# A decoder layer on one core: a prologue in halves and pieces, weight splits moved to GpSimd, and sixteen products of zeros at the start

## The reference

```
x = _layernorm(x + attn(x))            # 32 heads of 16, causal
x = _layernorm(x + xattn(x, ctx))      # 32 query heads in 8 groups, head size 128, rotary
x = _layernorm(x + ffn(x))             # 4-bit weights, 1376 wide, silu gate, result in float16

# attn: q, k, v = x @ W.T + b
scores = einsum('bhqd,bhkd->bhqk', q, k) / sqrt(16), causal
out = einsum('bhqk,bhkd->bhqd', softmax(scores), v) @ Wo.T + bo
# xattn: q = rope(query @ wq); k = rope(ctx @ wk); v = ctx @ wv
w = softmax(where(mask, einsum('bhgqd,bhkd->bhgqk', q, k) / sqrt(128), -1e9))
out = einsum(w, v) @ wo
# ffn: gate * sigmoid(gate) * up, gate = x @ Wg, up = x @ Wu, then @ Wd
```

## Time and profile before

| | us |
|---|---|
| median of 3 runs | 992.58 (988.86 to 994.84) |
| the profiled execution | 994.55 |
| its span in the trace | 992.7 |
| PE busy | 912.0 (92%) |
| DVE busy | 729.7 (74%) |
| ACT busy | 463.7 (47%) |
| POOL busy | 365.3 (37%) |

### The profile page before, as it was taken

One profiled execution on the slowest core, in us unless ns is written; L12 is line 12 of the kernel. 1 busy time (PEld: TensorE's weight loads), 2 busy tenths in 40 slices (PEclk: granted clock), 3 DMA queues, 4 the chain that ended last, 5 costly groups with the idle time before them and its releaser, 6 DMA issues.

```text
span 992.7 us, 17835 instructions
## 1 busy us (share of the span) xinstructions
PE 912.0 (92%) x6552; PEld 520.5 (52%) x6552; DVE 729.7 (74%) x1190; ACT 463.7 (47%) x1335; POOL 365.3 (37%) x330
## 2 busy tenths in 40 slices
PE   3876899888789999999999999999998989999997
PEld 2555677544345555545555555555554544444443
DVE  5685989877577877859787687787788655898343
ACT  3665788641145545535554454554545533333100
POOL 2152122103345444534554455446556230231011
PEclk9997999889999999999999999999999999999999
DMA  6634442210001101012002003004111010220001
GB/s 198 222 133 145 154 119 65 84 67 1 1 1 44 41 25 42 24 43 85 23 2 85 22 2 106 2 32 154 49 48 47 4 48 1 95 96 1 11 33 43
DMA packets 50535, 59.48 MB, mean 60 GB/s; under 512 B 5037, under 2 KB 35728, under 8 KB 50448
## 3 DMA queue, kind: packets, MB, share of 16 engines
q1 hardware_dynamic: 50448, 58.33, 18.2%
HBM read 51.96 MB, written 6.36 MB: 59 GB/s over the span
## 4 chain that ended last, share of the span: by engine, by line
PE 66%; DVE 13%; issue 9%; POOL 4%; ACT 4%; DMA 2%; SPq 1%; POOLq 0%; DVEq 0%; ACTq 0%
PE bank L292 19%; PE bank L293 19%; PE bank L294 19%; DVE rsin L873 3%; PE bank L1271 2%; ACT prob L691 1%; PE bank L1162 1%; POOL res L463 1%; DVE nmax L791 1%; PE bank L1261 1%; PE bank L1260 1%; PE bank L1259 1%; PE bank L1255 1%; DVE pTl L765 1%; ACT prob L575 1%
## 5 line engine op out<-in xcount | busy, mean ns | idle before, releaser
L470 POOL TENSOR_TENSOR rot<-rcos,rsin 128x512 f32<-128x512 f32 x80 | 101.3, 1266 | 123.2 <-DVE rsin L873 123.1
L482 POOL TENSOR_TENSOR pnrm<-prob,rden 128x512 f32<-128x512 f32 x64 | 66.5, 1040 | 125.0 <-DVE rden L933 124.9
L292 PE MATMUL bank<-aTh,xqh 128*128 128x512 f16 x256 | 98.2, 384 | 6.4 <-DVE aTl L765 3.7
L293 PE MATMUL bank<-aTl,xqh 128*128 128x512 f16 x256 | 98.1, 383 | 0.0
L530 ACT ACTIVATE pTh<-bank 128x512 f16<-128x512 f32 x128 | 78.5, 613 | 41.8 <-PE bank L1271 28.1
L294 PE MATMUL bank<-aTh,xql 128*128 128x512 f16 x256 | 97.9, 383 | 0.0
L294 PE MATMUL bank<-xoh,o2l 128*128 128x512 f16 x256 | 97.8, 382 | 0.0
L293 PE MATMUL bank<-xol,o2h 128*128 128x512 f16 x256 | 97.7, 382 | 0.0
L292 PE MATMUL bank<-xoh,o2h 128*128 128x512 f16 x256 | 97.6, 381 | 0.0
L610 ACT CAST q2h<-rot 128x512 f16<-128x512 f32 x64 | 39.5, 617 | 116.4 <-POOL rot L470 116.3
L575 ACT ACTIVATE prob<-bank,ebias 128x128 f32<-128x128 f32 x256 | 73.6, 382 | 42.3 <-DVE ebias L794 41.9
(11 more groups left out here) (159 smaller groups left out, 2454.0 us busy)
## 6 DMA issues: line engine op xcount, KB each, us to landing
tst<-tables SPq DMA_DIRECT2D x11, 768.0 KB, 5.5
xqs<-in_xwq SPq DMA_DIRECT2D x8, 1024.0 KB, 6.7
xos<-in_xwo SPq DMA_DIRECT2D x8, 1024.0 KB, 5.5
qst<-in_fq SPq DMA_DIRECT2D x11, 384.0 KB, 3.4
kstk<-stack SPq DMA_DIRECT2D x48, 64.0 KB, 2.3
qstk<-stack SPq DMA_DIRECT2D x24, 128.0 KB, 2.6
stT<-in_xT SPq DMA_DIRECT2D x4, 512.0 KB, 7.2
stT<-in_ctxT SPq DMA_DIRECT2D x1, 2048.0 KB, 8.1
```

The lines of the kernel that those rows point to most:

```text
L292: pe.matmul(out_ap, ah, bh, start=first, stop=False)
L293: pe.matmul(out_ap, ah, bl, start=False, stop=False)
L470: nc.gpsimd.tensor_tensor(rot[:, r % 2, :], rcos[:, r % 2, :], rsin[:, r % 2, :], ALU.add).then_inc(rope_rot, 1)
L482: nc.gpsimd.tensor_tensor(pnrm[:, v % 2, :].rearrange("p (h k) -> p h k", h=QH), prob[:, v % 2, :].rearrange("p (h k) -> p h k", h=QH), rd ...
```

## The change

The diff makes five groups of edits.

1. **Prologue.** The transposed x is loaded and split in halves of 512 columns (`load_x`, `x_split_hi`, `x_split_lo`), and the weights of keys, queries and values each have their own semaphore, so the first key products wait for the key weights and for one quarter of the first half at a time. The bias columns are loaded from ACT's queue. For block 0, ACT writes the high part of keys and queries straight from PSUM beside qkf, DVE makes the low part (`first_split_lo`), SP takes the keys through the scratch tensor and ACT the queries. The loads of the tables and the mask are issued after the keys of block 0, and DVE computes the tables and mbias in step 1 and no longer in step -8.
2. **Zero products.** POOL clears one half of pTh, and PE multiplies it sixteen times, 128 by 128 by 512, before its first step. The first `p1_hi` steps wait for them.
3. **Weight splits on POOL.** `split_piece` is three POOL instructions: scale the float32 tile in place, convert to the high part, subtract for the low part. POOL does so for the self attention's third and fourth weight sets (6 pieces), for wo (4), for the cross attention's query, key and value weights of groups 0 and 1 (12) and its output weights of group 0 (4): 26 pieces. ACT and DVE lose one instruction each for every piece. POOL's eight additions of bo move to steps 24 to 31, and its splits of keys and queries are interleaved by step.
4. **Self attention.** ebias is computed by ACT just before the exponentials and no longer by DVE; DVE's split of the values comes at the end of the same step, one step earlier than before.
5. **End of the cross attention.** The four transposes of res stand one step later, `gate_up(0)` one step earlier.

PE's list at the start, before: the products of keys wait for everything at once.

The diff, cut to what the list above names:

```diff
+IDLE = 16
...
-    plan += [(END - 6 + b, "t", (1, b)) for b in range(4)]
+    plan += [(END - 5 + b, "t", (1, b)) for b in range(4)]
...
-    qkv = {0: [24, 26, 28, 30, 32, 34], 1: [38, 40, 42, 44, 46, 48]}
-    out = {0: [50, 52, 54, 55], 1: [T0 + 2, T0 + 3, T0 + 4, T0 + 5]}
+    qkv = {0: [26, 28, 29, 30, 34, 36], 1: [38, 42, 44, 45, 46, 50]}
+    out = {0: [52, 53, 54, 58], 1: [T0 + 2, T0 + 3, T0 + 4, T0 + 5]}
...
+W1_SLOT = {(2, 0): 4, (2, 1): 5, (2, 2): 6, (3, 0): 20, (3, 1): 21, (3, 2): 22}
+WO1_SLOT = {0: 10, 1: 12, 2: 13, 3: 14}
+POOL_QKV, POOL_OUT = (0, 1), (0,)
...
-EARLY_GU = {END: [0], END + 1: [1], END + 3: [2], END + 5: [3]}
+EARLY_GU = {END - 1: [0], END + 1: [1], END + 3: [2], END + 5: [3]}
...
-GU_USE = {0: END + 1, 1: END + 2, 2: END + 4, 3: END + 6}
+GU_USE = {0: END, 1: END + 2, 2: END + 4, 3: END + 6}
...
+            def keep_first_keys():
+                sp.wait_ge(first_lo, 1)
+                for i, src in enumerate((k1h, k1l)):
+                    sp.dma_start(stack_d[0, i], src[:, :]).then_inc(k1_out, 16)
+
+            def bring_keys(j):
...
+                keep_rows(j, 0, k1_out, 2 * j - 1)
+                keep_rows(j, 2, q1_out, 2 * j)
+                if j >= 2:
+                    sp.wait_ge(s_psum, TILES1 * (j - 1))
+                bring_keys(j)
                 sp.wait_ge(q1_out, 32 * (j + 1))
...
+            def load_x(half):
+                cols = slice(half * HALF, (half + 1) * HALF)
...
+                    sp.dma_start(stT[:, k, cols], xT[k * P:(k + 1) * P, cols]).then_inc(x_in[half * NK + k], 16)
...
+            load_first_w1(0, wkT)
+            load_x(0)
+            load_first_w1(1, wqT)
+            load_first_w1(2, wvT)
+            load_x(1)
+            for dst, src in ((ident, ident_d), (tri_f, tri_d)):
+                sp.dma_start(dst[:, :], src).then_inc(early_in, 16)
             load_w1(1)
+            keep_first_keys()
+            bring_keys(0)
...
-            stack_rows(0)
+            sp.wait_ge(xT_lo, NHALF * NK)
             sp.dma_start(stT[:, :, :], ctxT.rearrange("(k p) t -> p k t", p=P)).then_inc(ctx_in, 16)
             stack_rows(1)
...
+            nc.gpsimd.memset(pTh[:, 0, :], 0.0).then_inc(idle_zero, 1)
             nc.gpsimd.memset(power[:, :], -0.5).then_inc(power_set, 1)
             pool.wait_ge(power_set, 1)
-            pool.wait_ge(early_in, 80)
+            pool.wait_ge(early_in, 32)
...
+                nc.gpsimd.tensor_tensor(res[:, b, :], res[:, b, :], bo_bc[:, :], ALU.add).then_inc(res_ready, 1)
...
+            def split_piece(hi, lo, src, lo_done):
+                nonlocal pieces_done
+                pieces_done += 1
+                nc.gpsimd.tensor_scalar(src, src, 2.0 ** E_W, None, ALU.mult).then_inc(piece_scaled, 1)
+                pool.wait_ge(piece_scaled, pieces_done)
+                nc.gpsimd.tensor_copy(hi, src).then_inc(piece_hi, 1)
+                pool.wait_ge(piece_hi, pieces_done)
+                nc.gpsimd.tensor_tensor(lo, src, hi, ALU.subtract).then_inc(lo_done, 1)
...
+            def pieces(t):
+                for (c, i), slot in W1_SLOT.items():
+                    if slot == t:
+                        w1_piece(c, i)
...
+            for t in range(FIRST, END + 7):
+                j, n, v = t // TILES1, t % TILES1, t - T0
+                if 0 < j + 2 < BLOCKS and n == 6:
+                    split_keys(j + 2)
+                if 0 < j + 1 < BLOCKS and n == 0:
+                    split_queries(j + 1)
+                pieces(t)
+                if 24 <= t < 24 + NB:
+                    add_bias(t - 24)
...
+                    act.wait_ge(first_lo, 1)
+                elif j >= 2:
+                    act.wait_ge(qk_lo, 2 * j - 3)
...
+                column = dict(scale=2.0 ** (E_QK - E_X - E_W), bias=bcols[:, 1, j // NHALF:j // NHALF + 1])
+                if j == 0:
+                    nc.scalar.activation(k1h[:, :], proj_bank(j, "k")[:, :], ACT.Identity, **column).then_inc(first_hi, 1)
+                nc.scalar.activation(qkf[:, 0, :], proj_bank(j, "k")[:, :], ACT.Identity, **column).then_inc(k1_f32, 1)
...
+                act.wait_ge(nmax_done, u + 1)
+                if u >= 2:
+                    act.wait_ge(exp_done, u - 1)
+                split_hi(ebias[:, u % 2, :], nmax[:, u % 2, :], -2 * E_QK - 2).then_inc(ebias_done, 1)
...
+                else:
+                    act.wait_ge(idle_done, 1)
...
+            def keep_first_queries():
+                act.wait_ge(first_lo, 2)
+                for i, src in enumerate((q1h, q1l)):
+                    act.dma_start(stack_d[0, 2 + i], src[:, :]).then_inc(q1_out, 16)
+
+            def bring_first_queries():
+                act.wait_ge(q1_out, 32)
+                for slot, part in enumerate((2, 2, 3)):
+                    act.dma_start(qstk[slot * ROWS:(slot + 1) * ROWS, 0, :, :],
+                                  stack_d[0, part].rearrange("(p r) t -> r p t", r=ROWS)).then_inc(stack_in[0], 16)
+
+            with nc.allow_non_contiguous_dma("bias columns"):
+                for i, src in enumerate((bq, bk, bv)):
+                    act.dma_start(bcol[:, i, :], src.rearrange("(c p) -> p c", p=P)).then_inc(bias_in, 16)
+            w1_split_hi(0, 0)
...
-            act.wait_ge(early_in, 80)
+                x_split_hi(0, k)
...
+            act.wait_ge(bias_in, 48)
             for i, e in enumerate((E_QK, E_QK, E_V1)):
                 split_hi(bcols[:, i, :], bcol[:, i, :], e).then_inc(scaled_bias, 1)
+            w1_split_hi(0, 2)
...
+                if t == FIRST + 3:
+                    for k in range(NK):
+                        x_split_hi(1, k)
                 if j + 1 < BLOCKS and n == 0 and t >= -TILES1:
                     q1_out_f32(j + 1)
+                if t == FIRST + 5:
+                    keep_first_queries()
...
-                dve.wait_ge(nmax_done, u + 1)
-                nc.vector.tensor_scalar(ebias[:, u % 2, :], nmax[:, u % 2, :], 2.0 ** (-2 * E_QK) / 4, None,
-                                        ALU.mult).then_inc(ebias_done, 1)
...
+            def first_split_lo(i):
+                dst, hi, done = ((k1l, k1h, k1_f32), (q1l, q1h, q1_f32))[i]
+                dve.wait_ge(done, 1)
+                dve.wait_ge(first_hi, i + 1)
+                nc.vector.tensor_tensor(dst[:, :], qkf[:, i, :], hi[:, :], ALU.subtract).then_inc(first_lo, 1)
...
-                if t == -TILES1:
+                if t == FIRST + 2:
+                    first_split_lo(0)
+                if t == FIRST + 3:
+                    for k in range(NK):
+                        x_split_lo(1, k)
+                if t == FIRST + 4:
+                    first_split_lo(1)
+                if t == 1:
                     tables()
                     dve.wait_ge(table_in, 96)
...
-                if before + 1 < BLOCKS and m == 4 and t - 1 > -TILES1:
-                    v1_split_lo(before + 1)
+                if j + 1 < BLOCKS and n == 4 and t > -TILES1:
+                    v1_split_lo(j + 1)
...
+                    if first:
+                        pe.wait_ge(xT_lo, k + 1)
...
+            pe.wait_ge(idle_zero, 1)
+            for i in range(IDLE):
+                last = pe_.matmul(bank[7][:, :], pTh[:, 0, 0:P], pTh[:, 0, :], start=True, stop=True)
+            last.then_inc(idle_done, 1)
```

164 lines of the change are left out of this document (90 added, 74 removed).

## The result

The changed kernel takes 975.68 us (median of 4 runs, 974.52 to 977.52), the kernel before 991.74 in the same session (988.86 to 994.84). The ratio is 0.984, with a 95% interval of 0.980 to 0.987. The forecast was 959.0, range 947 to 977: the sign and the range hold, but of the 35.8 us forecast only 16 to 19.5 came (19.5 between the two profiled spans, 992.7 and 973.2; 16 between the medians).

What follows compares the result with a forecast made beforehand. PE is full from 261 us on, so the first 261 us decide, with their waits on loads, POOL and DVE. Terms -9.0 + 4.0 - 15.8 - 1.0 - 6.0 - 4.0 - 4.0 = -35.8 from 994.55 give 959 us, range 947 to 977.

Steps and rivals of the forecast that it cites:

- The start, -9.0: Up to step 0: its scores start at 23.5 us, no longer 32.66; -9.0 us (-11.5 to -4.5).
- The tables, +4.0: Step 1: tables now ahead of tile 1's row maximum, DVE free at 30 instead of 26; +4.0 us (+1 to +7).
- Steps 8 to 16, -15.8: Self attention: the wait for res goes, PE's floor of 18.4 us replaces 34.2; -15.8 us (-17 to -8).
- Steps 16 to 21, -1.0: Self attention, at a clock of 0.84 before: saves 1.0 us.
- Steps 21 to 53, -6.0: Self attention: PE's floor of 73.6 replaces 81.6 us, less 2 for POOL's queue; -6.0 us (-8 to +4).
- Steps 53 to 72, -4.0: 11 ebias and three low parts come off DVE; -4.0 us (-8 to 0).
- the end, -4.0: Last transposes and pnrm: later transposes and earlier `gate_up(0)` fill PE's waits, part comes back; -4.0 us (-7 to 0).
- A: Rival: POOL late in every block, a piece costing 3.6 to 4.4 us; 974 us, chance 0.15.
- B: Rival: one tile's chain binds, blocks stay at 20.4 us with ebias on ACT; 970 us, chance 0.12.
- E: Rival: prologue does not shorten, bias columns and x fight, the 9 us are 2; 966 us, chance 0.05.
- D: Rival: denser PE keeps its clock, 7 us of steps 53 to 72 return; 950 us or less, chance 0.07.
- C: Rival: slower, POOL and the loop go in lockstep, from a 4.5 us piece on; 1001 us, chance 0.04.

Runs made afterwards that it cites:

- e3: The changed kernel with the table operations at steps 18 and 20 instead of step 1, their two stores behind group 0's weights; 975.81 us, ratio 0.984.
- e15: e9 with the context's four splits at steps 10, 14, 18 and 22 instead of 3, 7, 11 and 15; 962.08 us, ratio 0.969.
- e13: The changed kernel with only the first output-weight load moved behind block 5's rows and group 1's loads; 972.59 us, ratio 0.980.
- e2: The changed kernel with bias adds at steps 16 to 19, 32, 33, 35, 37 and the first output-weight load behind group 1's; 963.85 us, ratio 0.971.
- e11: The changed kernel with the end of the cross attention as in the kernel before; 979.59 us, ratio 0.987.
- e14: The changed kernel with only four of eight bias adds moved, from steps 28 to 31 to steps 16 to 19; 966.15 us, ratio 0.973.
- e6: e2 with the scaling of the row maximum (ebias) back on VectorE in the self attention; 975.71 us, ratio 0.982.
- e9: The changed kernel with table operations spread over steps 26 to 42, weight pieces from step 9, adds spread, group 1 and output-weight loads later; 962.65 us, ratio 0.970.
- e4: The changed kernel with the edits of e2 and e3 together; 966.48 us, ratio 0.975.

## Why the prediction was right and wrong

**The start, -9.0: right in mechanism, 1.5 too much.** The key rows were written at 13.3 as forecast, but landed at 17.75 and not 16.5, and the reads, issued by 20.5, at 25.2 and not 22.5: the last took 5.1 us, where the median of all such reads is 2.3. What held it no run separates. The chain behind the first weights and the write:

```profile
3.17 6.38 DMA w1s<-in_wqT
...
13.88 3.87 DMA stack<-k1l
```

The 0 for the zero products holds as far as can be told: 0.6 us at the key output, inside its bounds.

**The tables, +4.0: the step that failed second.** The tables cost 4.3 against the changed kernel's own profile (e3), some 4 over all traces, about as forecast. The steps took 7.5 longer in the two profiles. What I left out is the context, whose load the change puts behind all that block 0 needs: its splits are worth 2 to 3 us there (e15). That the +7.5 is near my upper bound of 7 is luck, for that bound was for the tables alone.

**Steps 8 to 16, -15.8: right, 2.2 too much.** The wait for res went, and nothing read back was late. Step 12 to 13 took 5.9 us against 3.8 for the same step of the next block: v1l and a cTl both stand ahead of its row maximum. It took 5.8 before, with a w1l of 1.37 us and a cTl of 2.29 beside the adds.

**Steps 16 to 21, -1.0:** they got 0.55 longer; PE waited 0.9 us in all at the full clock where it had been full at 0.84. Why the full clock gave nothing back there stays open.

**Steps 21 to 53, -6.0: the step that failed, by the 2 us for the queue at step 40.** PE's floor was forecast at 18.4 and came as 18.2 (steps 24 to 32, at a clock of 1.00), which is -8.8 against my -8.0. The queue at step 40 was seen and priced at 2 us (0 to 12); it cost 10.4. GpSimd's piece made some of the difference: the scale took 1.49 us, above the dearer of my two rows (1.41), the piece 3.4 and not 3.0, and the queries were split 33.3 us behind step 24 and not about 30 (113 less 64.5 and 18.4). From there to their read-back it took 11.4 us and not 9.5, for the rows landed behind the 1 MB load that I had on the list but counted as issue time alone (the load's place is worth 3.2 us, e13). PE was ready for step 40 at 127.0, 0.9 us sooner behind step 24 than forecast. And 1.5 more went behind the wait, where the clock is low. The Trainium skill (GPSIMD Engine Reference, Elementwise — side-by-side cycle accounting) would have had the scale at about 0.44 us, an estimate from its 1.03 cycles an element at 1.2 GHz, dispatch left out; the trace decides, 1.49 for float32 out and 0.61 for the cast to float16.

**Steps 53 to 72, -4.0, and the end, -4.0:** -3.7 and -4.4. The first is not well known: kernels with the same lists there (e2, e3, e11 to e14) take 77.2 to 79.8 us for it, and the clock is 0.91 before and after. e11 gives the end 3.9 in time.

**The rivals.** A (GpSimd late in every block) came within 2 us by its price, 974, and that is luck: one block was late and not each, by adds and pieces together, and the subtraction that A had at more than 1.16 us took 1.16 in the loop. B (the chain of one tile binds, with ebias now on ScalarE) is false: the blocks run at PE's floor, and with ebias back on VectorE (e6) they don't. E is out, step 0 moved 7.5 us. D and C did not come. The measured 975.7 lies in my range only because I had stretched it from 967 to 977 for A and B, neither of which came.

**A version that beats both.** e2, e9 and e15 take 962 to 964 us, 12 to 14 less than the changed kernel, with intervals of 0.967 to 0.975 that lie wholly below its 0.980; among the three I can tell no difference.

## What to carry to other kernels

A queue that is sure to be late somewhere should be laid out row by row with its round trip, up to the first instruction that waits for it: 2 us on paper were 10 here, since three things came on top of GpSimd's lateness: a load behind which the next store stands, the round trip, and the clock that falls in the wait. Look in the block where several kinds of side work fall due together, and spread them before moving anything else. And what is gained at the start counts only from the place at which the next late thing lies: here the tables and the context took the start's gain in the changed kernel, and with the tables gone a read-back took it at step 16 in e4. And work moved off a busy engine onto its neighbour can slow what stays: ebias, 0.17 us alone, took 0.51 beside GpSimd's pieces.

## What was not expected of the hardware

- GpSimd's scaling of 128x512 float32 in place takes 1.49 us, more than its two-input subtraction (1.16) and more than twice its cast (0.61).
- An instruction of VectorE's on four elements takes 0.52 us beside GpSimd's adds, three times its own 0.17, while 512 elements from PSUM beside the same adds take their usual 0.68.
- In the cross attention, where TensorE has waits of some us, kernels with the same instructions are granted different clocks. The changed kernel and e2 run the same lists there. Their first four cross tiles, in this order:

```profile
246.14:284.36 38.22, 32.08 (x183) 16.86 (x182) 26.74 (x44) 15.71 (x53) 17.07 (x17) 0.92 0.00 1
```

```profile
233.18:268.60 35.42, 29.28 (x183) 16.23 (x182) 26.64 (x43) 15.71 (x52) 17.08 (x17) 1.00 0.00 1
```

  The mean clock is 0.92 in one and 1.00 in the other, and that goes with 2.8 us of 38. e9 is at 0.93 there and takes 37.9 us; it is 1.6 us ahead of e2 at step 53 and 3.7 behind at the fifth cross tile. (Between step 53 and the first cross tile e9 has more of GpSimd's pieces than e2, 43.8 us of work against 32.1, so that part of the loss may be theirs.) Gains of 2 to 3 us ahead of that stretch are therefore hard to see in the time, and why the clock falls one way or the other stays open; no run was made for it.
